# Layer 1 attention: low score products on 64 partition rows, two heads side by side, without zero tiles

## What is computed

```python
def reference(x, ...):
    x = x + _L0_conv_ref(_ln_c(x), ...)             # attention, 12 heads of 32, relative positions
    t = _to_tokens(x)
    t = t + _L0_ffn_ref(_ln_t(t), ...)              # 8 experts, top 2, inner width 384
    x = _from_tokens(t, x)
    x = x + _L1_conv_ref(_ln_c(x), w_qkv, w_out)    # neighbourhood attention
    t = _to_tokens(x)
    t = t + _L1_ffn_ref(_ln_t(t), ...)              # shared expert + 8 experts, top 2, inner 768
    return _from_tokens(t, x)

def _natten2d(q, k, v, ksize):                      # inside _L1_conv_ref, ksize 7
    kg = k[:, :, ih[:, None, :, None], iw[None, :, None, :], :]
    logits = einsum('nhije,nhijabe->nhijab', q / sqrt(32), kg)
    return einsum('nhijab,nhijabe->nhije', softmax(logits), vg)
```

## Time and profile before

| | |
|---|---|
| median of 3 runs | 1144.03 us (1144.02 to 1146.78) |
| the profiled execution | 1143.17 us, span of its instructions 1141.6 us |
| PE, DVE, ACT, POOL busy | 89%, 45%, 28%, 28% of the span |
| chain that ended last, by engine | PE 71%, DVE 9%, DMA 8%, ACT 5% |
| gathers of layer 0 and addition to X | 540 to 569 us |
| chunks of attention in layer 1 | 598 to 721 us |

### The profile page before, as it was taken

One profiled execution on the slowest core, in us unless ns is written; L12 is line 12 of the kernel. 1 busy time (PEld: TensorE's weight loads), 2 busy tenths in 40 slices (PEclk: granted clock), 3 DMA queues, 4 the chain that ended last, 5 costly groups with the idle time before them and its releaser, 6 DMA issues.

```text
span 1141.6 us, 13662 instructions
## 1 busy us (share of the span) xinstructions
PE 1011.7 (89%) x4561; PEld 587.9 (51%) x4562; DVE 510.3 (45%) x898; ACT 321.9 (28%) x492; POOL 323.9 (28%) x281
## 2 busy tenths in 40 slices
PE   6999999999980799997278888979999999999998
PEld 3755555554440466664136656558554554455554
DVE  4566687888562255553534465671111111111114
ACT  3514544554611122121014545241111111111100
POOL 5514677777735001000510000254000000000004
PEclk9999999999995799999598999999999999999999
DMA  8599308000077236411733100523344424411005
GB/s 293 148 284 279 85 14 172 1 1 1 2 269 260 70 138 221 152 55 50 206 96 73 43 15 2 193 78 118 131 152 160 158 81 175 175 51 42 14 27 159
DMA packets 47114, 132.45 MB, mean 116 GB/s; under 512 B 6865, under 2 KB 25817, under 8 KB 46808
## 3 DMA queue, kind: packets, MB, share of 16 engines
q1 hardware_dynamic: 32424, 67.41, 20.4%
q0 software_dynamic: 14640, 64.36, 15.8%
HBM read 89.88 MB, written 30.87 MB: 106 GB/s over the span
## 4 chain that ended last, share of the span: by engine, by line
PE 71%; DVE 9%; DMA 8%; ACT 5%; issue 4%; POOL 3%; SPq 1%; POOLq 0%; DVEq 0%; ACTq 0%
PE PS L1667 21%; PE PS L1688 10%; PE PS L1471 6%; PE PS L1520 5%; PE PS L1397 5%; PE PS L1640 4%; DMA Wd<-in_Wd_r 4%; PE PS L1501 3%; DVE nmax_part L1156 3%; PE PS L1503 3%; PE PS L1714 3%; ACT QB L946 2%; DMA bd<-in_bd 2%; PE PS L1451 2%; DVE exp_acc L1188 2%
## 5 line engine op out<-in xcount | busy, mean ns | idle before, releaser
L1667 PE MATMUL PS<-Wgu,xbT 128*128 x690 | 285.5, 556 | 9.2 <-DMA Wd<-in_Wd_r 5.4
L1667 PEld LDWEIGHTS PS<-Wgu,xbT 128*128 128x128 f32 x690 | 127.9, 191 | 127.6 <-issue 114.8
L962 ACT ACTIVATE expS<-PS 128x1024 f32<-128x1024 f32 (+3 forms) x156 | 135.5, 878 | 135.2 <-PE PS L1503 134.0
L1688 PE MATMUL PS<-Wd,hidT 128*128 x414 | 143.1, 491 | 1.5 <-DVE hidT L1297 0.8
L798 POOL TENSOR_TENSOR exp_acc<-exp_acc,expS 128x512 f32<-128x512 f32 (+1 forms) x65 | 124.5, 1915 | 47.6 <-ACT expS L962 46.8
L1471 PE MATMUL PS<-KS,QA 128*128 128x512 f32 (+2 forms) x288 | 109.3, 426 | 18.7 <-DVE nmax L1156 6.8
L1501 PE MATMUL PS<-QA,KS 128*128 128x512 f32 (+3 forms) x312 | 116.9, 380 | 9.0 <-ACT QB L946 9.0
L1156 DVE TENSOR_REDUCE nmax_part<-PS 128x1 f32<-128x512 f32 x160 | 103.6, 684 | 46.0 <-PE PS L1471 45.2
L1503 PE MATMUL PS<-QB,KS 128*128 128x512 f32 (+3 forms) x312 | 111.7, 364 | 0.0
L1688 PEld LDWEIGHTS PS<-Wd,hidT 128*128 128x128 f32 x414 | 78.7, 191 | 57.6 <-issue 14.4
L1471 PEld LDWEIGHTS PS<-KS,QA 128*128 128x128 f32 x288 | 52.2, 191 | 83.1 <-DVE nmax_part L1156 44.6
(11 more groups left out here) (170 smaller groups left out, 1177.2 us busy)
## 6 DMA issues: line engine op xcount, KB each, us to landing
Wgu<-in_Wgu POOLq DMA_DIRECT2D x8, 1152.0 KB, 6.3
Wgu<-in_Wg_r POOLq DMA_DIRECT2D x8, 1152.0 KB, 6.4
Wgu<-in_Wu_r POOLq DMA_DIRECT2D x8, 1152.0 KB, 8.5
Wd<-in_Wd_r POOLq DMA_DIRECT2D x8, 1152.0 KB, 10.8
xb<-block_rows_in SPq DMA_DIRECT2D x46, 192.0 KB, 2.4
block_rows_out<-yb SPq DMA_DIRECT2D x46, 192.0 KB, 1.9
part_rows<-parts SPq DMA_DIRECT2D x2, 3072.0 KB, 17.9
Wd<-in_Wd POOLq DMA_DIRECT2D x8, 576.0 KB, 7.1
```

What stands on the lines that cost most here:

```text
L962: act.activation(exp_tile(layer, c, unit)[:, pair, :].rearrange("p (b n) -> p b n", b=2)[:, :, lo:hi], PS[:, 2 * pair:2 * pair + 2, lo:hi] ...
L1667: last = pe.matmul(PS[:, 3 * par + lo // BANK, 0:n], xbT[:, par, kc, :], Wgu[layer][:, bass.ds(s, 1), kc, lo:lo + n], start=kc == 0, stop= ...
L1688: last = pe.matmul(PS[:, 7, 0:C], hidT[layer][:, par, i, :], Wd[layer][:, bass.ds(s, 1), i, :], start=i == 0, stop=i == m.IC - 1)
```

## The change

1. In layer 1 the rows of KS and QA are turned for the odd heads: the low part of k lies in rows 0 to 31, the one-hot and mask rows are swapped (`place_turned`), and the high part of k lies in rows 96 to 127. For an even head the low product then needs rows 0 to 63 alone, for an odd one rows 64 to 127.
2. QB of layer 1 has room for two heads in one column block (even head in rows 0 to 63, odd in 64 to 127), so it is half as wide and has no zero rows. `zero_rows` and its DMAs (2 stores to DRAM, 2 fills of 1 MB) are gone.
3. `scores` in layer 1 makes both high products of a pair and then both low products, each on 64 rows: tile 64 x 128 at row 0, and at row 64.
4. The fill of QA11 with the mask (1 MB) is now issued behind the placing of q for chunk 0, not before it. Turned fills take three DMAs in place of one.

Layer 0 keeps its order. The core of the diff:

```diff
-        QB.append([at("QB10", [P, G, T], 0, F32R), at("QB11", [P, G, T], 2 * STACK, F32R)])
+        QB.append([at("QB10", [P, G // 2, T], 0, F32R), at("QB11", [P, G // 2, T], 2 * STACK, F32R)])
...
-        zero_rows = nc.dram_tensor("zero_rows", [2 * D, T], F32, kind="Internal").ap()
...
-        A_DMAS = [[17, 7, 6], [10, 9, 8]]
-        B_DMAS = [[16, 4, 4], [5, 5, 4]]
+        A_DMAS = [[17, 7, 6], [14, 11, 8]]
+        B_DMAS = [[16, 4, 4], [4, 4, 4]]
...
+        def low_rows(layer, g):
+
+            if layer == 0:
+                return slice(0, P)
+            return slice(0, D) if g % 2 == 0 else slice(3 * D, P)
+
+        def shift_rows(layer, g):
+
+            if layer == 0:
+                return slice(D, D + 1)
+            return slice(D, 2 * D) if g % 2 == 0 else slice(2 * D, 3 * D)
+
+        def low_half(g):
+
+            return slice(0, 2 * D) if g % 2 == 0 else slice(2 * D, P)
...
+            def place_turned(dst, rows, done):
+
+
+                place_same(dst[D:3 * D, 0:G:2], rows, done)
+                place_same(dst[D:2 * D, 1:G:2], rows[D:2 * D], done)
+                place_same(dst[2 * D:3 * D, 1:G:2], rows[0:D], done)
...
-            place_same(KS[1][0][D:3 * D], key_rows[1], a_in[0])
-            place_same(QA[1][0][D:3 * D], mask_rows, a_in[0])
+            place_turned(KS[1][0], key_rows[1], a_in[0])
+            place_turned(QA[1][0], mask_rows, a_in[0])
             routed(0)
-
-            place_same(QB[1][0][2 * D:P], zero_rows, b_in[0])
-            place_same(QA[1][1][D:3 * D], mask_rows, a_in[1])
-            place_same(QB[1][1][2 * D:P], zero_rows, b_in[1])
 
             def stack_direct(c):
 
                 s = c % 2
                 for lo in (0, D * 3):
                     place_direct(QA[1][s][lo:lo + D], q_part(1, c, False), "qk", a_in[s])
-                place_direct(QB[1][s][0:D], q_part(1, c, True), "qk", b_in[s])
+                for g in range(G):
+                    place(QB[1][s][low_rows(1, g), g // 2], q_part(1, c, True)[D * g:D * g + D].bitcast(F32), b_in[s])
 
             sp.wait_ge(job_dve, job_number(1, "q", 0))
             stack_direct(0)
             check(a_in[0], A_DMAS[1][0])
             check(b_in[0], B_DMAS[1][0])
+            place_turned(QA[1][1], mask_rows, a_in[1])
...
-                    for dst, src in ((KS[1][0][0:D], k_part(1, 0, False)), (KS[1][0][3 * D:P], k_part(1, 0, True))):
+                    for lo in (False, True):
                         for g in range(G):
-                            pool.dma_start(dst[:, g, :].bitcast(F32), src[D * g:D * g + D].bitcast(F32)).then_inc(k_in[1], 16)
+                            rows = slice(0, D) if lo == (g % 2 == 1) else slice(3 * D, P)
+                            pool.dma_start(KS[1][0][rows, g, :].bitcast(F32),
+                                           k_part(1, 0, lo)[D * g:D * g + D].bitcast(F32)).then_inc(k_in[1], 16)
...
-                        last = act.activation(QB[layer][c % 2][D:D + rows, g, half * BANK:(half + 1) * BANK],
+                        column = g if layer == 0 else g // 2
+                        last = act.activation(QB[layer][c % 2][shift_rows(layer, g), column, half * BANK:(half + 1) * BANK],
...
+                    queries = slice(half * BANK + lo, half * BANK + hi)
+
+                    def high_product(j):
+                        g = 2 * pair + j
+                        pe.matmul(PS[:, 2 * pair + j, lo:hi], KS[layer][c % 2][:, g, kt * P:(kt + 1) * P],
+                                  QA[layer][c % 2][:, g, queries], start=True, stop=False)
+
+                    if layer == 0:
+                        for j in range(2):
+                            g = 2 * pair + j
+                            high_product(j)
+                            last = pe.matmul(PS[:, g, lo:hi], KS[0][c % 2][:, g, kt * P:(kt + 1) * P],
+                                             QB[0][c % 2][:, g, queries], start=False, stop=True)
+                        last.then_inc(score_psum, 1)
+                        return
+                    for j in range(2):
+                        high_product(j)
                     for j in range(2):
                         g = 2 * pair + j
-                        keys = KS[layer][c % 2][:, g, kt * P:(kt + 1) * P]
-                        queries = slice(half * BANK + lo, half * BANK + hi)
-                        pe.matmul(PS[:, 2 * pair + j, lo:hi], keys, QA[layer][c % 2][:, g, queries],
-                                  start=True, stop=False)
-                        last = pe.matmul(PS[:, 2 * pair + j, lo:hi], keys, QB[layer][c % 2][:, g, queries],
-                                         start=False, stop=True)
+                        last = pe.matmul(PS[:, g, lo:hi], KS[1][c % 2][low_half(g), g, kt * P:(kt + 1) * P],
+                                         QB[1][c % 2][low_half(g), g // 2, queries], start=False, stop=True)
```

More of the change, by code:

```diff
@@ L557, in place_same @@
             def place_same(dst, rows, done):
-                place(dst, rows.rearrange("p (a t) -> p a t", a=1).broadcast_to([rows.shape[0], G, T]), done)
+                place(dst, rows.rearrange("p (a t) -> p a t", a=1).broadcast_to([rows.shape[0], dst.shape[1], T]), done)
+            def place_turned(dst, rows, done):
+                place_same(dst[D:3 * D, 0:G:2], rows, done)
+                place_same(dst[D:2 * D, 1:G:2], rows[D:2 * D], done)
+                place_same(dst[2 * D:3 * D, 1:G:2], rows[0:D], done)
             def check(done, dmas):
@@ L644, in _ @@
             sp.dma_start(mask_rows[:, :], mask_const[D:3 * D, :]).then_inc(const_stored, 16)
-            for n in range(2):
-                sp.dma_start(zero_rows[D * n:D * n + D, :], mask_const[0:D, :]).then_inc(const_stored, 16)
             sp.wait_ge(k_stored, 16 * 2)
@@ L656, in _ @@
             stack_from_rows(2)
-            sp.wait_ge(const_stored, 16 * 6)
+            sp.wait_ge(const_stored, 16 * 4)
             sp.wait_ge(proj_dve, NT)
             sp.dma_start(Wqkv[1][:, :, :], w_qkv1.rearrange("(k p) n -> p k n", p=P)).then_inc(wq_in[1], 16)
-            place_same(KS[1][0][D:3 * D], key_rows[1], a_in[0])
-            place_same(QA[1][0][D:3 * D], mask_rows, a_in[0])
+            place_turned(KS[1][0], key_rows[1], a_in[0])
+            place_turned(QA[1][0], mask_rows, a_in[0])
             routed(0)
-            place_same(QB[1][0][2 * D:P], zero_rows, b_in[0])
-            place_same(QA[1][1][D:3 * D], mask_rows, a_in[1])
-            place_same(QB[1][1][2 * D:P], zero_rows, b_in[1])
             def stack_direct(c):
```

## The result

| | before | after |
|---|---|---|
| median | 1144.85 us (1144.02 to 1146.78) | 1153.12 us (1152.35 to 1154.23) |
| profiled execution | 1143.17 us, span 1141.6 | 1153.85 us, span 1152.3 |
| ratio | | 1.0074, 95% interval 1.0058 to 1.0091 |

The changed kernel is slower by 0.74%; the prediction, 1148.3 us and slower by 0.4%, had the sign, and the time lies in its range. It lies 4.8 us above the value, though (+8.3 us against the median of before where +4.3 was forecast), and that has to be found.

A forecast was written before the change was run, and what follows sets the result against it. DMA was taken to bound the gathers of layer 0 and PE the attention of layer 1. 1143.17 - 6.1 + 10.4 = 1147.5 us against the profiled execution, 1148.3 against the median; range 1140 to 1155.

The forecast's parts named there:

- the two stretches: Attention of layer 1, taken as bound by PE, and the gathers of layer 0, taken as bound by DMA.
- Part 1: Gathers of layer 0: without fills beside them the fourth token tile is added sooner, -6.1 us (bounds -5.0 and -6.1).
- A change of tile: Scores of layer 1: entering 64-row tiles costs 0.21 us, returning 0.22; a pair nets +0.26 at 384 queries, +0.31 at 256.
- The whole term: Low products in layer 1 attention: 8.3 + 0.5 + 1.4 + 0.2 = +10.4 us, upper end 11.4.
- That 64 rows cost nothing: Rival, layer 1 scores: PE enters 64-row tiles without emptying, so pairs save time; 1131.6 us, chance 0.17.
- the first rival: No cost for 64 rows, 1131.6 us, chance 0.17; sign turns where a pair's two changes cost about 0.3 us.
- Serial loads: Rival, layer 1 scores: second low weight load waits for the first, 0.11 us per pair, +4.2; 1152.5 us, chance 0.25.
- That the low products don't run side by side: Rival, layer 1 scores: no slot is saved in a pair, +5.8; 1154.1 us, chance 0.07.
- The slow gathers: Rival, gathers of layer 0: the fills aren't what slows them, so part 1 gains nothing; 1154.4 us, chance 0.05.
- The turned fills ahead of the mixture of layer 0: SP's queue before the scatter: four more issues, 2.6 us of SP, hidden by its wait for the scatter; costed at nothing.
- The 1 us each way for PE's clock after the shorter rest: Range allowance after the layer 0 gathers, since how soon PE regains its clock couldn't be read from the trace.

The follow-up runs named there:

- fills_behind_q: Kernel before with its three 1 MB fills (zeros, mask, zeros) issued behind the placing of q for chunk 0, scores as before; 1136.80 us, ratio 0.9941.

## Why the prediction was right, and where it was off

**What bounds the two stretches** was read rightly. The gathers bound by DMA: the share fell from 0.85 to 0.38 and they came sooner. PE bounds attention: every change of tile was paid.

**Part 1, -6.1 us** (bounds -5.0 and -6.1): -6.2 in the trace, -6.35 between the medians of `fills_behind_q` and before. The nearest row without traffic was the right one to take.

**A change of tile: 0.10 lost and 0.11 of open load on the way in, 0.11 and 0.11 on the way back.** The rows of after show 0.10 and, back, 0.09, each with the open load. The pair of 384 costs +0.22 (predicted 0.26), the pair of 256 +0.27 (0.31), a half 1.42 to 1.51 (1.66). **The whole term: +9.4 in the first pair of traces, +10.0 over all of them, +10.4 predicted.** That the total comes this close is in part luck: four of the halves cost less than forecast, and the first one 2.8 us, by a longer stretch at the lower clock that no term had. The Trainium skill, page "TensorEngine Tiling (Array Packing)", section Tiling Modes, says that a change of mode drains TensorE; this trace agrees, with 0.09 to 0.10 us for each change.

**The rivals.** That 64 rows cost nothing falls at 1.09 us from pair to pair. The Trainium skill, page "TensorE: Matmul & The Clock Gate", Part 3, Measured speedup vs the span model, gives the span of packed tiles without a charge for entering them. Taken as the whole cost, as in this rival, it does not hold in this trace, where the two changes of a pair take 0.4 us. Serial loads fall at two loads in 0.19 us. That the low products don't run side by side falls with the same two pairs, which fit one slot and not two. The slow gathers fall at 3.04 us. The point named for the first rival held in direction: the sign is decided by whether two changes cost more than 0.3 us; they cost 0.4. The time alone would not have decided: 1153.1 us lies nearer to serial loads (1152.5), to products that don't run side by side (1154.1) and to slow gathers (1154.4) than to the forecast of 1148.3. The range held the result because it had been drawn wide enough for these rivals; that the forecast's mechanism was the right one is shown by the traces.

**The step that failed** is in Part 1: "The turned fills ahead of the mixture of layer 0 add four issues, 2.6 us of SP, which then waits for the scatter anyway." This counts the issues on SP's queue and not what the transfers do to others. The same DMA engines carry the expert weights at that moment; with the fills cut in three they moved 297 in place of 351 GB/s, the third load was awaited 13.3 in place of 10.1 us, and no slack covered it, since weights and routing had been ready within 0.5 us of each other. The term was 0 and is +3.2 us in the first pair of traces, +3.6 in the mean of all. With 3.6 the sum would have been 1151.9, and 1153.1 was measured. The row that would have warned stood in the profile: POOL waiting 10.10 us for a landing, just ahead of the scatter and in the chain of waits, with the DMA engines busy 0.90 of the time. The mistake is the odder as Part 1 rests on the same effect 200 us later.

The 1 us each way for PE's clock after the shorter rest covers the 0.5 us by which the scores start later than the shift alone gives; whether the clock is the cause of these isn't shown. It wasn't meant for the clock in the first half of chunk 0, some 1.4 us.

## What to carry to other kernels

A product on half the rows saves PE nothing by itself; it saves a slot where two run side by side, each entry and each exit costs about 0.2 us, and with four such products to a change it just broke even here. Where a DMA is cut into pieces or reshaped, cost it at the transfers that run beside it as well as at its queue, and look for whoever waits for those. Work that is grouped to save changes must not be what another engine's next step hangs on.

## What the runs showed of the hardware

- Two weight loads of 64 x 128 for different row halves run together, 0.19 us for both, and so do the two products, 0.44 us for both by the record.
- A step between 128-row and 64-row tiles empties TensorE for 0.09 to 0.10 us and lays the next load of 0.11 us open, in both directions.
- With such a step at each product the granted clock had a mean of 0.61, 0.72 and 0.66 in three stretches of 30 us and 1.00 in a fourth, with PE busy 95 to 96% of each by the record (28.63 to 28.87 of 30 us). The profiled execution took 63 us more than with half the steps; by estimate 28 of them are the steps at full clock and the rest is the clock.
- Behind the first wait for the copied maxima the granted clock was at its lower level for 3.4 us with whole-array products of scores (six traces) and for 6.8 us with low products on 64 rows in each pair (five traces).
- Two fills of 1 MB, each cut into one piece of 64 partitions and two of 32, hold back a large load beside them: it is awaited 13.3 to 13.7 us in place of 9.9 to 10.1. Cut into two pieces of 64 partitions they don't (9.88). With the fills elsewhere it is 6.64 us.
